# Self-attention probabilities divided by their sums on VectorE before they are turned, in the loop of a two-layer transformer kernel

## The reference

```python
scores = jnp.einsum('bnqhd,bnkhd->bnhqk', q, k) / jnp.sqrt(jnp.float32(D)).astype(h.dtype)
attn = jax.nn.softmax(scores, axis=-1)
o = jnp.einsum('bnhqk,bnkhd->bnqhd', attn, v).reshape(B, L, C)
```

## Time and profile before

| | |
|---|---|
| median of three runs | 1450.2 us |
| profiled execution | 1446.67 us, its span 1444.8 us |
| busy share of the span | DVE 70%, ACT 58%, POOL 30%, weight loads 83% |
| granted TensorE clock | 0.996 of full speed |
| one pass of the loop | about 82 to 90 us |
| chain that ended last | PE 86%, DVE 9%, issue 2%, others 1% or less |

### The profile page before, as it was taken

One profiled execution on the slowest core, in us unless ns is written; L12 is line 12 of the kernel. 1 busy time (PEld: TensorE's weight loads), 2 busy tenths in 40 slices (PEclk: granted clock), 3 DMA queues, 4 the chain that ended last, 5 costly groups with the idle time before them and its releaser, 6 DMA issues.

```text
span 1444.8 us, 30134 instructions
## 1 busy us (share of the span) xinstructions
PE 1411.6 (98%) x9805; PEld 1196.0 (83%) x9805; DVE 1015.4 (70%) x4628; ACT 840.4 (58%) x2555; POOL 427.7 (30%) x613
## 2 busy tenths in 40 slices
PE   7999999999999999999999999999999999999997
PEld 5778888888888888888888788888888878887886
DVE  3586859587695868769595786959587685958642
ACT  3474475757566384756757366674857547574433
POOL 1314132233324232331334132233234313222302
PEclk9999999999999999999999999999999999999999
DMA  7620000000000000010010000000010000000000
GB/s 244 193 76 2 1 7 20 6 29 9 19 30 16 1 1 26 2 33 3 20 37 1 15 2 16 11 21 15 9 49 1 16 1 5 5 2 8 1 4 11
DMA packets 27340, 34.98 MB, mean 24 GB/s; under 512 B 3324, under 2 KB 22448, under 8 KB 26929
## 3 DMA queue, kind: packets, MB, share of 16 engines
q1 hardware_dynamic: 27185, 33.07, 7.2%
HBM read 28.83 MB, written 4.22 MB: 23 GB/s over the span
## 4 chain that ended last, share of the span: by engine, by line
PE 86%; DVE 9%; issue 2%; SPq 1%; ACT 1%; DMA 1%; POOL 0%; DVEq 0%; ACTq 0%; POOLq 0%
PE bank L955 13%; PE bank L910 13%; PE bank L979 11%; PE bank L962 7%; PE bank L919 6%; PE bank L783 6%; PE bank L769 5%; PE bank L842 4%; PE bank L894 4%; PE bank L830 4%; DVE knocked L2187 3%; PE bank L822 2%; PE bank L740 2%; PE bank L754 2%; PE bank L804 1%
## 5 line engine op out<-in xcount | busy, mean ns | idle before, releaser
L910 PE MATMUL bank<-hB,Wm 128*128 128x256 f32 x1024 | 242.3, 383 | 2.2 <-ACT hB L1356 2.2
L910 PEld LDWEIGHTS bank<-hB,Wm 128*128 128x128 f32 x1024 | 190.6, 190 | 33.3 <-issue 7.0
L955 PE MATMUL bank<-nxT,W1nx 128*128 128x256 f32 x896 | 211.5, 382 | 0.0
L1395 ACT ACTIVATE prob<-bank,rmax 128x128 f32<-128x128 f32 x512 | 180.3, 433 | 28.2 <-DVE rmax L2135 28.2
L1746 POOL TENSOR_TENSOR scores<-scores,M 128x308 f32<-128x308 f32 x128 | 94.4, 737 | 319.4 <-DVE knocked L2187 317.0
L1402 ACT ACTIVATE probT<-bank 128x512 f32<-128x512 f32 (+1 forms) x256 | 140.0, 618 | 82.2 <-PE bank L894 76.4
L979 PE MATMUL bank<-W2p,gT 128*128 128x256 f32 x768 | 183.2, 381 | 3.0 <-DVE acc L2266 1.9
L955 PEld LDWEIGHTS bank<-nxT,W1nx 128*128 128x128 f32 x896 | 165.7, 190 | 22.9 <-issue 2.8
L979 PEld LDWEIGHTS bank<-W2p,gT 128*128 128x128 f32 x768 | 141.2, 190 | 23.8 <-issue 2.8
L1434 ACT ACTIVATE tbs<-bank,b1half 128x256 f32<-128x256 f32 x128 | 60.7, 474 | 143.2 <-PE bank L910 102.3
L1450 ACT ACTIVATE tbs<-bank,betaH 128x256 f32<-128x256 f32 x224 | 95.6, 489 | 82.7 <-PE bank L962 82.7
(11 more groups left out here) (232 smaller groups left out, 2712.3 us busy)
## 6 DMA issues: line engine op xcount, KB each, us to landing
Wm_g<-in_L_xcond_w_m_dram SPq DMA_DIRECT2D x4, 1024.0 KB, 5.4
W1ev<-in_L_xcond_e_w_dram SPq DMA_DIRECT2D x6, 512.0 KB, 7.3
x<-in_x_dram SPq DMA_DIRECT2D x16, 128.0 KB, 2.3
x<-in_x_dram SPq DMA_DIRECT2D x32, 64.0 KB, 2.3
Wm<-in_L_xcond_w_m_dram SPq DMA_DIRECT2D x1, 2048.0 KB, 8.5
out_dram<-acc SPq DMA_DIRECT2D x16, 128.0 KB, 1.7
out_dram<-acc SPq DMA_DIRECT2D x32, 64.0 KB, 2.0
batch_rows<-row_store SPq DMA_DIRECT2D x4, 384.0 KB, 3.7
```

The lines of the kernel that those rows point to most:

```text
L910: m = pe.matmul(bank_of(name)[:, half * UT:(half + 1) * UT], Wm1[:, k, c:c + P], hB[:, k, :], start=(k == 0), stop=(k == CB - 1))
L955: pe.matmul(bank_of(name)[:, n * UT:(n + 1) * UT], W1nx[:, k, c0 + n * P:c0 + (n + 1) * P], nxT[:, k, :], start=(n == 0 and k == 0), stop= ...
L1395: m = act.activation(prob[:, s, i, :], psum[s][:, i * P:(i + 1) * P], ACT.Exp, bias=rmax[:, t, s * HPS + i:s * HPS + i + 1], accum_out=rsu ...
```

## The change

In the loop (units 2 and later) each slot's exponentials are divided by their sums before they are turned. VectorE gets eight `a_weigh(t, s)` in a pass: it waits for the slot's exponentials, inverts the slot's four sums (128 x 4) and multiplies `prob[:, s]` (128 x 512) in place by the inverses, broadcast along the 128 keys. `a_turn_probs` waits for that. In return step 7 above goes away in the loop: the inversion of all sums, GpSimd's spreading, TensorE's four turnings of it with ScalarE's copy; and `a_normalise` for `pv` becomes a plain copy `a_values_out`. In TensorE's list, the first tile's turnings come later: the first behind `b_first_nx("h20")` instead of in front of it, and the last two behind `b_second(0, (2, 3))` instead of in front of it, directly ahead of the second tile's scores. In VectorE's list `ln_stats(2)` moves from behind `b_silu("h10")` to between the second tile's second and third weighing. The prologue and the last two passes without self-attention keep the old way; `r1` is a job of bank 0 there alone (`PRO_ONLY`).

```diff
+PRO_ONLY = {"r1": 0}
...
             def a_turn_probs(t, s, u):
                 wait_drained(pe, f"s{t}{s}", u)
+                if weighs_early(t, u):
+                    pe.wait_ge(weighted, weighed(t, s, u))
                 for i in range(HPS):
                     m = pe.transpose(psum[s][:, i * P:(i + 1) * P], prob[:, s, i, :], ident[:, :])
...
                 b_second(0, (0, 1), b)
+                b_first_nx("h20", 2 * RH, b)
                 a_turn_probs(0, 0, a)
-                b_first_nx("h20", 2 * RH, b)
                 a_turn_probs(0, 1, a)
+                b_second(0, (2, 3), b)
                 a_turn_probs(0, 2, a)
                 a_turn_probs(0, 3, a)
-                b_second(0, (2, 3), b)
                 a_scores(1, range(SLOTS), a)
...
-                a_turn_inverses("r1", "pv", a)
                 a_values(1, a)
...
                 b_tanh_first("h20", hE[:, 0], 0, 8, b)
-                a_copy_inverses("r1", "pv", a)
...
-                a_spread("pv", a)
...
+            def a_weigh(t, s, u):
+
+                g = slice(s * HPS, (s + 1) * HPS)
+                wait_drained(dve, f"s{t}{s}", u)
+                dve.reciprocal(rinv[:, t, g], rsum[:, t, g]).then_inc(slot_inverted, 1)
+                dve.wait_ge(slot_inverted, weighed(t, s, u))
+                dve.tensor_tensor(prob[:, s], prob[:, s], rinv[:, t, g].rearrange("p (i a) -> p i a", a=1).to_broadcast([P, HPS, P]),
+                                  ALU.mult).then_inc(weighted, 1)
+
+            def a_values_out(dst, u):
+
+                wait_full(dve, "pv", u)
+                dve.tensor_copy(dst.rearrange("p f t -> p (f t)"), bank_of("pv")[:, :]).then_inc(drained[JOB["pv"][0]], 1)
...
                 a_max(0, (3,), a)
+                a_weigh(0, 0, a)
                 b_route_norm(b)
+                a_weigh(0, 1, a)
                 a_residual(xc, xc, "co", c)
+                a_weigh(0, 2, a)
+                a_weigh(0, 3, a)
                 b_silu("h10", hE[:, 1], 0, b)
-                wait_drained(dve, "co", c)
-                ln_stats(2, xc, c)
                 b_mix(0, b)
                 a_max(1, (0,), a)
                 a_max(1, (1,), a)
                 a_max(1, (2,), a)
                 a_max(1, (3,), a)
                 b_silu("h11", hE[:, 1], 2, b)
-                a_invert_sums(a)
+                a_weigh(1, 0, a)
+                a_weigh(1, 1, a)
+                wait_drained(dve, "co", c)
+                ln_stats(2, xc, c)
+                a_weigh(1, 2, a)
+                a_weigh(1, 3, a)
                 ln_apply(2, xc, xnB, c)
-                a_normalise("pv", oT, a)
+                a_values_out(oT, a)
```

More of the change, by code:

```diff
@@ L79 @@
 DEFERRED = {"e2": "m6", "g2": "y01"}
-for _jobs in BANK_JOBS:
+PRO_ONLY = {"r1": 0}
+for _bank, _jobs in enumerate(BANK_JOBS):
     _n = 0
     for _name, _u in PRO_JOBS:
-        if _name in _jobs:
+        if _name in _jobs or PRO_ONLY.get(_name) == _bank:
             PRO_ORDER[_name, _u] = _n
@@ L101 @@
         _n += 1
+for _name, _bank in PRO_ONLY.items():
+    JOB[_name] = (_bank,)
 def before(name, u):
@@ L122 @@
 TANH_ORDER = [f"m{j}" for j in range(HJ)] + FIRST_ORDER
+EARLY = [0, 1]
 TOPK_ORDER = [("a", 0, 0), ("a", 0, 1), ("b", 0, 0), ("a", 0, 2), ("a", 0, 3), ("b", 0, 1), ("b", 0, 2), ("a", 1, 0), ("b", 0, 3), ("a", 1, 1), ("b", 1, 0), ("a", 1, 2), ("b", 1, 1), ("a", 1, 3), ("b", 1, 2), ("b", 1, 3)]
@@ L298, in bass_pixart_experts @@
         row_max = sem("row_max")
-        sums_inverted, kept_inverted = sem("sums_inverted"), sem("kept_inverted")
+        sums_inverted, slot_inverted, kept_inverted = sem("sums_inverted"), sem("slot_inverted"), sem("kept_inverted")
+        weighted = sem("probabilities_weighted")
         spread_x = sem("kept_inverses_spread")
@@ L347, in bass_pixart_experts, with weighs_early, weighed @@
         HEADS = [(s, j, e) for s in range(SLOTS) for j in range(PAIR) for e in range(PAR)]
+        def weighs_early(t, u):
+            return u >= 2 and t in EARLY
+        def weighed(t, s, u):
+            return (u - 2) * (len(EARLY) * SLOTS) + EARLY.index(t) * SLOTS + s + 1
         def head(s, i):
@@ L1393, in a_exp @@
                 for i in range(HPS):
-                    h = head(s, i)
+                    h = s * HPS + i if weighs_early(t, u) else head(s, i)
                     m = act.activation(prob[:, s, i, :], psum[s][:, i * P:(i + 1) * P], ACT.Exp,
```

## The result

The changed kernel took 1464.66 us (median of 4 runs, 1460.23 to 1464.69) against 1450.48 us for the kernel before on the same chip (4 runs, 1448.33 to 1450.88). The ratio is 1.0085, 95% interval 1.0074 to 1.0097: slower by 14.2 us, against +12.6 forecast.

A forecast was written before the change was run, and what follows sets the result against it. TensorE was taken to bound the kernel, its loop passes lasting as long as their matmuls. 14 x (0.93 - 0.44) = +6.9, 11 x 0.05 = +0.6 and 3 x 1.7 = +5.1 gave +12.6: 1462.8 us, range 1453 to 1471.

The forecast's parts named there:

- In the loop TensorE stands still nowhere: Claim about the kernel before: no TensorE waits in the loop, so a pass takes as long as its matmuls.
- The hand-over in front of the scores: Second tile's scores wait for ScalarE's copy of the last turning: 0.93 us a pass, bounds 0.7 and 1.2.
- The turnings removed: Four turnings of the inverses leave TensorE's list in each of 14 passes: 0.44 us each pass, 6.2 us.
- The first tile's multiplications: VectorE's four, partly held by GpSimd's bias work: the fourth just in time, at worst 0.3 us.
- The second tile in ordinary passes: In 11 passes the last turning waits for its multiplication 0 to 0.1 us, taken as 0.05, up to 0.3.
- The gate's passes: In three passes GpSimd's gate holds VectorE's second-tile multiplications: TensorE waits 1.7 us a pass, bounds 0 and 2.2.
- The sum: All terms over the passes together: +12.6 us; low ends +3.6, high ends +20.5.
- What would show it: Profile signs: 14 scores' waits of 0.8 to 1.0 us; VectorE about 90 us busier, GpSimd 10 less, TensorE about 6 less.
- Rival 1: The turnings taken out are the whole effect, copies free in time: 6.2 us faster, 1444.0 us; chance 0.07.
- Rival 2: Scores' wait of 0.3 to 0.6 us, nothing in the gate's passes: the two cancel, about 1450 us; chance 0.07.
- Rival 3: VectorE late in every pass, TensorE losing 1.7 us more each: 24 us on top, about 1487 us; chance 0.07.
- Rival 4: New gaps slow TensorE's clock, each costing 2 us of half speed: 14 us more, 1477 us; chance 0.03.

The follow-up runs named there:

- e1: The kernel before with only TensorE's new order in the first tile, no division of the exponentials on VectorE: 1461.09 us, ratio 1.0083.
- e2: The changed kernel with VectorE's multiplication over only 4 of the 128 keys of each head, all waits kept: 1456.08 us, ratio 1.0048.
- e3: The kernel before's order with no division by the sums in the loop and step 7's work left out: 1446.54 us, ratio 0.9975.
- e4: The changed kernel with TensorE's old order in the first tile: 1479.8 us, ratio 1.0204.
- e6: The changed kernel with `b_route_norm`, which starts GpSimd's bias work, behind the first tile's four weighings: 1475.32 us, ratio 1.0196.
- e7: The changed kernel with `b_route_norm` behind the first tile's weighings and h11's evidence matmuls directly before the second tile's scores: 1472.23 us, ratio 1.0169.
- e12: Like e9, but GpSimd's five bias operations start behind `b_silu("h10")`, between the tiles, and the sixth follows `rstd_of(2)`: 1453.01 us, ratio 1.0028.
- e9: The changed kernel with h11's evidence matmuls before the second tile's scores, `ln_stats(2)` behind the last weighing, GpSimd's bias work behind both tiles: 1463.19 us, ratio 1.0104.
- e5: The changed kernel with h11's evidence matmuls moved between the first tile's last turning and the second tile's scores: 1460.48 us, ratio 1.0087.

## Why the prediction was right

**The kernel before.** "In the loop TensorE stands still nowhere" is not so: it has four short waits there, three of 0.27 us for VectorE's `scores` and the 0.22 at 415.12 of the earlier trace rows, together 1.0 us in 14 passes. They change nothing in the forecast, but the stretch where they stand is the one that differs from pass to pass.

**The hand-over in front of the scores**, 0.93 us forecast: right. e1 and e2 measure 0.90. The hand-over itself, from the copy's end to the scores, was taken as 0.15 and is 0.14 in e1: the last copy ends at 191.07 and the scores start at 191.21. The 0.05 of the lower bound is in no run, and with it the terms give 0.8, not the 0.7 used for the range.

**The turnings removed**, 0.44 forecast: 0.44 in each pass, 6.1 us. That TensorE loses part of it elsewhere (+0.7 us in the changed kernel, +1.0 in e3) was taken as nothing.

**The first tile's multiplications**: the pattern was right (0.69, 1.55, 0.73, 1.55 us; the fourth held until GpSimd's third operation is over), the price was taken as nothing with 0.3 at worst. The turnings run 0.22 us longer, the wait behind them is 0.05 shorter (0.78 against 0.83), and the place costs 1.08 us against e2's 0.90: 0.18 in every pass, 2.6 us. This is the term that was missed.

**The second tile in ordinary passes**, 0.05 forecast: nothing there; the four multiplications take 0.69 us each and the three last turnings run through without a gap.

**The gate's passes**, 1.7 us forecast: mis-sized. The second tile costs 1.03 us there. The last turnings start 1.00 us late (795.51 against 793.64 + 0.87). Each multiplication lost 0.32 us beside the gate's operations of 0.7 us, the middle of the 0.2 to 0.5 used, but of the four only three lost any.

**The sum**: 12.6 for the hand-over, 2.6 for the first tile's multiplications, 3.1 for the gate's passes, -6.1 for the turnings, +0.7 elsewhere: 12.8 us by the unrounded figures of the table, which is the loop's +12.8. The forecast's +12.6 lacks the 2.6 and the 0.7 and has 2.0 too much for the gate's passes, 0.6 for the second tile and 0.4 for the hand-over. So part of its closeness is luck; the mechanism and its largest term are not. The measured medians are 14.2 us apart; what goes beyond the loop is mostly the start, below.

**What would show it.** The 14 waits came with 0.8 us each, the gate's passes with one listed wait of 0.5 instead of 1 to 2 us. VectorE's +113.6 us against +90: the 112 multiplications took 937 ns instead of 692, 27 us more. GpSimd was to be 10 us less busy and was 19.4 more. The spreading taken out is worth 11.2, as forecast, but the instructions that stay take longer beside VectorE, since the time in which an instruction is held counts as busy; the prediction had counted that on VectorE alone. TensorE's busy time rose by 4.8 us where a fall of 6 was forecast: the 0.16 us ahead of each wait counts as busy, and the prologue ran at a lower clock; this number was not traced further.

**The rivals.** Rival 1 (faster) is what e3 shows, a gain of 5.2 us that the waits outweigh. Rival 2, the two cancelling, needed a wait below 0.6 us in front of the scores; it cost 0.90. Rival 3, VectorE late in every pass, is not the changed kernel but e4, e6 and e7, and its price of 10 to 13 us above the changed kernel was half of the 24 given. Rival 4, a falling clock in the loop, did not come.

**The prologue.** The 5 us more at the start are the granted clock, not waits. It is 0.91 before and 0.83 after in 20 to 40 us, 0.92 and 0.91 in 60 to 80, 1.00 and 0.83 in 100 to 120: together 0.26 of 20 us, or 5.2 us. The stretch 100 to 120 us of before, and behind it of after (us, then busy us of PE, PEld, DVE, ACT, POOL, clock, DMA share, GB/s):

```profile
100.00:120.00 20.00, 19.23 (x215) 17.10 (x216) 7.03 (x19) 9.94 (x27) 2.64 (x8) 1.00 0.17 54
```

```profile
100.00:120.00 20.00, 18.11 (x187) 15.71 (x186) 6.93 (x19) 11.38 (x37) 2.42 (x6) 0.83 0.17 54
```

In the 14 profiled executions the loop started at 123.95 to 129.33 us, with no order by what was changed: 125.05 in e1 and 126.43 in e12, 129.11 in e9. One of the four runs of the changed kernel was 4.4 us shorter than the others. In e12 the clock was 0.91 in 1380 to 1400 and in 1420 to 1440 us, against 1.00 in the changed kernel, and the stretch behind the loop 3.0 us longer than before's. These are taken for chance of the single execution, which is not shown; whether a kernel's arrangement makes them likelier isn't settled, and the effect is as large as the 3.6 us by which e12 stands above before.

## What to carry to other kernels

An order written by hand hides hand-overs. Where the last use of a buffer and its next writer become neighbours on the critical engine, the whole latency of producer, copy and semaphore is exposed (here 1.42 us from the last turning to the scores, 0.90 of it lost), however idle the engine between them is.

Work given to an engine "with idle time" is priced by who shares its path to memory: the same multiplication cost 0.69 or 1.55 us depending on what GpSimd did. Moving the other side only moves the meeting, so lay both engines' two-input instructions beside each other for the whole pass, and put GpSimd's work beside VectorE's reads of PSUM.

Before moving work to make room, measure the ceiling with the work left out. Here it was 5.2 us of the loop, 0.25% by e3's ratio, and none of the eight rearrangements e5 to e12 got below the kernel before.

Compare stretch by stretch, not by totals: e1 and the changed kernel lose the same 12.6 and 12.8 us, for different reasons.

## What the runs showed of the hardware

**VectorE and GpSimd hold each other for whole instructions, and both sides pay.** A multiplication of 128 x 512 with two SBUF inputs: 0.69 us alone, 1.55 beside GpSimd's 128 x 512, 1.01 beside its 128 x 256, 0.30 on average for 128 x 16 (e2). GpSimd's bias additions: 1270 ns on average before, 1554 in the changed kernel.

**An instruction with one tensor input from SBUF is held too.** `ln_apply`, a float32 TENSOR_SCALAR from SBUF to SBUF, takes 0.74 us for a pair alone, as here in the changed kernel:

```profile
797.09 0.74 DVE L2128 TENSOR_SCALAR xnB<-x,mv,rstd 128x256 f32<-128x256 f32 x2 [1.73 <-POOL rstd L1752]
```

Beside GpSimd it took 1.56 in the kernel before and 2.08 to 2.17 us in e9. The expectation of e9 had named `b_silu("h20")` and the residual, not this. The Trainium skill ("SBUF — State Buffer", section "Who interferes with whom") does list `tensor_scalar` among the operations that can take the shared ports, in a mode that needs both of them; these rows agree that it is held, and do not show the mode. The same section says that a VectorE reduction never contends; the maxima of 2.48 us in e12 agree.
